# A third stack buffer, and the second of two layer norms computed from the first one's input, in a fused attention and expert kernel

## The reference

```python
# block A: x = x + difference attention to the context; layer norm without weights
h  = _layernorm(x)                       # "B1", this h is also the residual's base
# token block, entered with h
n1 = _layernorm(h, ln1_g, ln1_b)         # "B": a norm of something already normed
h  = h + softmax(causal(q(n1) k(n1)^T / 4)) v(n1) Wp + bp      # 16 heads, T = 1024
n2 = _layernorm(h, ln2_g, ln2_b)         # "M"
h  = h + top-2-of-8 experts(n2)          # each expert 256 -> 1024 -> 256 with gelu
# later blocks: C (attention), L1 (ternary), D, L2 (butterfly weights), E, F (routed attention)
```

## Time and profile before

| | us |
|---|---|
| median of three runs | 4305.14 |
| the three runs | 4296.96, 4305.14, 4316.94 |
| the profiled execution | 4313.47 |
| its span from first to last instruction | 4311.7 |
| mean granted TensorE clock | 0.915 |

### The profile page before, as it was taken

One profiled execution on the slowest core, in us unless ns is written; L12 is line 12 of the kernel. 1 busy time (PEld: TensorE's weight loads), 2 busy tenths in 40 slices (PEclk: granted clock), 3 DMA queues, 4 the chain that ended last, 5 costly groups with the idle time before them and its releaser, 6 DMA issues.

```text
span 4311.7 us, 55263 instructions
## 1 busy us (share of the span) xinstructions
PE 3544.3 (82%) x21566; PEld 1905.3 (44%) x21566; DVE 2280.4 (53%) x5155; ACT 1523.4 (35%) x2282; POOL 353.6 (8%) x270
## 2 busy tenths in 40 slices
PE   5388878878878849999779798797987988888889
PEld 2233333343343338888435334453344543444534
DVE  8865466466466436666463443724446344364343
ACT  3134424334333423443342323433225332244322
POOL 6000001000100124444000000000000000000000
PEclk8688988988988869999999899899999999999989
DMA  3221231131040168777210302102120122101130
GB/s 120 84 69 16 71 94 16 53 111 16 20 145 9 27 152 221 225 224 206 55 35 21 56 12 51 35 1 39 49 51 16 21 33 55 45 16 26 26 62 11
DMA packets 206360, 279.59 MB, mean 65 GB/s; under 512 B 100816, under 2 KB 164962, under 8 KB 190116
## 3 DMA queue, kind: packets, MB, share of 16 engines
q1 hardware_dynamic: 189065, 255.41, 22.5%
q0 software_dynamic: 17024, 20.53, 2.4%
HBM read 199.30 MB, written 75.14 MB: 64 GB/s over the span
## 4 chain that ended last, share of the span: by engine, by line
PE 52%; DVE 25%; DMA 8%; ACT 7%; issue 4%; SPq 2%; POOL 1%; DVEq 0%; ACTq 0%; another core or an unknown queue 0%
PE ps L860 6%; PE ps L1365 5%; DVE max_parts L2018 4%; PE ps L807 4%; PE ps L809 4%; PE ps L808 4%; PE ps L996 3%; PE ps L956 3%; PE ps L1211 3%; PE ps L1218 3%; DMA x_tokens<-scr_x_normalised,arena 2%; PE ps L979 2%; DVE minus_max_context L2154 2%; ACT arena L1535 2%; PE ps L1139 2%
## 5 line engine op out<-in xcount | busy, mean ns | idle before, releaser
L860 PE MATMUL ps<-ternary_W,ident 128*128 128x512 f16 x2420 | 741.3, 417 | 123.7 <-ACT arena L1596 36.8
L2018 DVE TENSOR_REDUCE max_parts<-ps 128x1 f32<-128x512 f32 (+3 forms) x768 | 387.2, 552 | 210.4 <-PE ps L959 161.0
L1467 ACT ACTIVATE arena<-ps 128x256 f32<-128x256 f32 (+7 forms) x512 | 319.1, 650 | 465.1 <-PE ps L979 288.3
L860 PEld LDWEIGHTS ps<-ternary_W,ident 128*128 128x128 f16 x2420 | 239.3, 104 | 466.5 <-issue 144.1
L956 PE MATMUL ps<-k_stack,q_stack 96*128 96x512 f16 (+3 forms) x768 | 265.5, 381 | 76.6 <-DVE max_parts L2018 33.9
L1535 ACT ACTIVATE arena<-ps 77x1024 f32<-77x1024 f32 x192 | 190.4, 1016 | 273.8 <-PE ps L1131 268.8
L1938 DVE CAST arena<-arena 128x256 f16<-128x256 f32 (+3 forms) x424 | 160.8, 379 | 235.2 <-ACT arena L1633 151.1
L2432 DVE TENSOR_REDUCE max_parts<-ps 128x1 f32<-128x512 f32 x256 | 170.6, 689 | 171.9 <-PE ps L1338 169.3
L979 PE MATMUL ps<-q_stack,k_stack 98*128 98x512 f16 (+3 forms) x768 | 236.1, 353 | 30.4 <-ACT arena L1467 27.1
L1940 DVE TENSOR_TENSOR arena<-arena 128x256 f16<-128x256 f32 (+3 forms) x424 | 246.1, 580 | 14.6
L1697 ACT ACTIVATE arena<-ps 128x1024 f32<-128x1024 f32 x128 | 130.5, 1023 | 337.1 <-PE ps L1354 337.1
(11 more groups left out here) (433 smaller groups left out, 7259.4 us busy)
## 6 DMA issues: line engine op xcount, KB each, us to landing
arena<-scr_expert_weights SPq DMA_DIRECT2D x52, 1024.0 KB, 7.4
k_stack<-scr_expert_weights SPq DMA_DIRECT2D x26, 1024.0 KB, 7.6
q_stack<-in_exp_W SPq DMA_DIRECT2D x16, 1024.0 KB, 10.6
scr_expert_weights<-k_stack SPq DMA_DIRECT2D x16, 1024.0 KB, 4.9
q_stack<-scr_q SPq DMA_DIRECT2D x120, 128.0 KB, 3.9
scr_q<-arena SPq DMA_DIRECT2D x48, 256.0 KB, 2.9
k_stack<-scr_q SPq DMA_DIRECT2D x72, 128.0 KB, 4.1
scr_q<-arena SPq DMA_DIRECT2D x16, 512.0 KB, 4.2
```

The source lines that it names most:

```text
L860: pe.matmul(s[:, 0:CH], ident[:], Wq1[:, 0, 0:CH], start=True, stop=True)
L1467: act.activation(PR[:, n % NP, kt * P:T], slot(L, "ST", g, kt, j)[:, kt * P:T], ACT.Exp).then_inc(*did("act", L, "exp", g, kt, j))
L2018: dve.tensor_reduce(mpart[:, j * NT + t, c:c + 1], slot(L, "S", g, t, j, c)[:, 0:n], AX, ALU.max).then_inc(*frees("dve", L, "S", g, t, j, c))
```

## The change

It has three parts.

1. A third buffer of stacks: `Wexp` serves as its query half and `RT` as its key half. Group g uses buffer g % 3. The stack of group 2 is loaded straight after those of groups 0 and 1, ahead of the first `max_rows`; the stack of group 3 waits for the last `ST` of group 0.
2. Because `Wexp` and `RT` are overwritten, both (1 MB each) are stored to DRAM at the head of batch 0, ahead of the first expert loads in SP's list, and loaded again in phase 1 behind the weights of tiles 0 to 2. Constant rows of the third buffer are loaded once.
3. `norm_twice` replaces both calls of `norm`. The mean of a normed row is zero and its variance is v / (v + eps), so B needs no statistics of `H`: two small products, one more square root, reciprocal and product give a scale, and `XN["B"]` is computed from `X`. Its eight tiles are written first, the eight of `H` afterwards, ahead of `x_affine` in DVE's list.

```diff
+        stack_q = [QS[:, 0], QS[:, 1], Wexp[...].bitcast(F16)...]
+        stack_k = [KS[:, 0], KS[:, 1], RT[...].bitcast(F16)...]
...
             def stacks(L, own, g):
-                buf = g % 2
-                if g >= 2:
-                    sp.wait_ge(*of("pe", L, "ST", g - 2, NT - 1 if own else 0, GH - 1))
+                buf = g % 3
+                if g >= 3:
+                    sp.wait_ge(*of("pe", L, "ST", g - 3, NT - 1 if own else 0, GH - 1))
...
                 sp.wait_ge(*of("st_q1", L))
                 sp.wait_ge(*of("st_k1", L))
+                stacks(L, True, 2)
                 max_rows(L, 0)
...
-                    if g + 2 < NG:
-                        stacks(L, True, g + 2)
+                    if g + 3 < NG:
+                        stacks(L, True, g + 3)
...
             for b in range(NB):
+                if b == 0:
+                    sp.dma_start(d_up, Wexp[...]).then_inc(*did("st_l2", 0))
+                    sp.dma_start(d_down, RT[...]).then_inc(*did("st_l2", 1))
...
+                if b == 0:
+                    sp.wait_ge(*of("st_l2", 1))
+                    sp.dma_start(stack_q[2][48:MROW], A["c_qs"][:, 0])...
+                    sp.dma_start(stack_k[2][48:MROW + 2], A["c_ks"][:, 0])...
...
             for i in range(3):
                 tile_table(i)
                 tile_weights(i)
+            sp.dma_start(Wexp[...], d_up).then_inc(*did("ld_l2", 0))
+            sp.dma_start(RT[...], d_down).then_inc(*did("ld_l2", 1))
...
+            def norm_twice():
+                var2, rstd2, rboth = sm[:, 136:144], sm[:, 144:152], sm[:, 152:160]
+                for t in range(NT):
+                    dve.wait_ge(*of("dve", "B1", "bn", t))
+                    dve.bn_aggr(mv[:, t], stats[:, t])...
+                dve.wait_ge(*of("act", "B1", "sd"))
+                dve.reciprocal(rstd[:], sd[:])...
+                dve.tensor_tensor(var2, rstd[:], rstd[:], ALU.mult)...
+                dve.tensor_tensor(var2, var2, mv[:, :, 1], ALU.mult)...
+                dve.wait_ge(*of("act", "B", "sd"))
+                dve.reciprocal(rstd2, sd[:])...
+                dve.tensor_tensor(rboth, rstd[:], rstd2, ALU.mult)...
+                for N, dst, scale in (("B", XN["B"], rboth), ("B1", H, rstd)):
+                    for t in range(NT):
+                        dve.tensor_scalar(dst[:, t], X[:, t], mv[:, t, 0:1], scale[:, t:t + 1], ALU.subtract, ALU.mult)...
...
-                norm("B1", X, H)
+                norm_twice()
+                x_affine("B")
                 dve.wait_ge(*of("dve", "B1", "xn", NT - 1))
-                norm("B", H, XN["B"])
-                x_affine("B")
                 own_attention("B0", H, "M")
```

More of the change, by code:

```diff
@@ L646, in _ @@
                 led.phase, led.batch = 0, b
+                if b == 0:
+                    sp.dma_start(d_up, Wexp[:, :, :].rearrange("p k n -> p (k n)")).then_inc(*did("st_l2", 0))
+                    sp.dma_start(d_down, RT[:, :, :].rearrange("p m d -> p (m d)")).then_inc(*did("st_l2", 1))
                 for i in range(2):
@@ L721, in _ @@
                 tile_weights(i)
+            sp.dma_start(Wexp[:, :, :].rearrange("p k n -> p (k n)"), d_up).then_inc(*did("ld_l2", 0))
+            sp.dma_start(RT[:, :, :].rearrange("p m d -> p (m d)"), d_down).then_inc(*did("ld_l2", 1))
             sp.dma_start(KX[:MROW + 2], A["c_kx"]).then_inc(*did("ld_const", 0))
@@ L944, in own_attention @@
                     if g is not None:
-                        buf = g % 2
+                        buf, mbuf = g % 3, g % 2
                     if kind == "S":
@@ L950, in own_attention @@
                             pe.wait_ge(*of("ld_const", 2))
+                            if g == 2 and led.batch == 0:
+                                pe.wait_ge(*of("ld_const3", 1))
                         keys = (t + 1) * P
@@ L955, in own_attention @@
                             on_edge = c * CH + n == keys
-                            mm = pe.matmul(s[:, 0:n], QS[0:MROW, buf, j, t * P:(t + 1) * P], KS[0:MROW, buf, j, c * CH:c * CH + n],
+                            mm = pe.matmul(s[:, 0:n], stack_q[buf][0:MROW, j, t * P:(t + 1) * P], stack_k[buf][0:MROW, j, c * CH:c * CH + n],
                                            start=True, stop=not on_edge)
@@ L970, in own_attention @@
                             busy(s, 2 if g else 12)
-                            pe.wait_ge(*of(f"ld_m{buf}", L, g, 1))
+                            pe.wait_ge(*of(f"ld_m{mbuf}", L, g, 1))
                         q0_ = kt * P
@@ L978, in own_attention @@
                             edge = a == q0_
-                            mm = pe.matmul(o, KS[0:MROW + 2, buf, j, kt * P:(kt + 1) * P], QS[0:MROW + 2, buf, j, a:(c + 1) * CH], start=True, stop=not edge)
+                            mm = pe.matmul(o, stack_k[buf][0:MROW + 2, j, kt * P:(kt + 1) * P], stack_q[buf][0:MROW + 2, j, a:(c + 1) * CH], start=True, stop=not edge)
                             if edge:
@@ L1404, in _, with norm_std @@
             batch_end(act, "act")
-            def norm_std(N):
+            def norm_std(N, variance=mv[:, :, 1]):
                 act.wait_ge(*of("dve", N, "mv"))
-                act.activation(sd[:], mv[:, :, 1], ACT.Sqrt, bias=epsc[:, 0:1], scale=1.0).then_inc(*did("act", N, "sd"))
+                act.activation(sd[:], variance, ACT.Sqrt, bias=epsc[:, 0:1], scale=1.0).then_inc(*did("act", N, "sd"))
             def both(slot_):
@@ L1643, in _ @@
                 norm_std("B1")
-                norm_std("B")
+                norm_std("B", sm[:, 136:144])
                 x_affine("B", "ln1_g", "ln1_b")
@@ L1924, in both @@
                 return slot_.rearrange("p (k c) -> p k c", k=KD)
+            def norm_twice():
+                var2, rstd2, rboth = sm[:, 136:144], sm[:, 144:152], sm[:, 152:160]
+                for t in range(NT):
+                    dve.wait_ge(*of("dve", "B1", "bn", t))
+                    dve.bn_aggr(mv[:, t], stats[:, t]).then_inc(*(step("B1", "mv") if t == NT - 1 else step("B1", "ag", t)))
+                dve.wait_ge(*of("act", "B1", "sd"))
+                dve.reciprocal(rstd[:], sd[:]).then_inc(*step("B1", "rstd"))
+                dve.wait_ge(*of("dve", "B1", "rstd"))
+                dve.tensor_tensor(var2, rstd[:], rstd[:], ALU.mult).then_inc(*step("B", "squares"))
+                dve.wait_ge(*of("dve", "B", "squares"))
+                dve.tensor_tensor(var2, var2, mv[:, :, 1], ALU.mult).then_inc(*step("B", "mv"))
+                dve.wait_ge(*of("act", "B", "sd"))
+                dve.reciprocal(rstd2, sd[:]).then_inc(*step("B", "rstd"))
+                dve.wait_ge(*of("dve", "B", "rstd"))
+                dve.tensor_tensor(rboth, rstd[:], rstd2, ALU.mult).then_inc(*step("B", "both"))
+                dve.wait_ge(*of("dve", "B", "both"))
+                for N, dst, scale in (("B", XN["B"], rboth), ("B1", H, rstd)):
+                    for t in range(NT):
+                        dve.tensor_scalar(dst[:, t], X[:, t], mv[:, t, 0:1], scale[:, t:t + 1], ALU.subtract, ALU.mult).then_inc(*step(N, "xn", t))
             def x_lo(N):
```

14 lines of the change are left out of this document (10 added, 4 removed).

## The result

| | before | after |
|---|---|---|
| median, four runs of each | 4311.04 | 4240.45 |
| lowest and highest | 4296.96, 4320.47 | 4234.47, 4251.26 |
| profiled execution | 4313.47 | 4234.47 |
| its span | 4311.7 | 4232.7 |
| mean granted TensorE clock | 0.915 | 0.924 |

The ratio is 0.9838, with a 95% interval of 0.9816 to 0.9859: between 61 and 79 us less, 71 by the medians. The forecast was 4244, from a sum of -61.5, which lies at the edge of that interval.

What follows compares the result with a forecast made beforehand. PE, busy 82% of the span, was taken as the bound. -51 - 14 + 3 + 0.5 = -61.5 us takes the profiled 4313.5 to 4252, a median near 4244; own range 4230 to 4258, 8 in 10 for 4226 to 4268.

Steps and rivals of the forecast that it cites:

- Part 1: Third stack buffer, phase 0: all eight late stack waits go, with the slow clock behind them; about -51 us.
- the eight stretches: First ST to PV at kt = 2 around the late stack waits; 148.9 us in sum, forecast 12 to 13 each.
- The control: Group 0's same steps with the stack already there, 11.95 us; eight make 95.6, a difference of 53.3 us.
- the dip: Low clock from group 0's quiet end, at three of the eight groups; stays, for about 0.7 us each.
- One or two stack waits below 1 us: Waits of S for stack loads in phase 0: one or two left, instead of 10 with 31.9 us.
- Part 2: Norms B1 and B in four batches: both halves split 4.0 us sooner, -16, taken as about -14 us.
- Part 3: Saving and restoring the weights: +3 us at batch 0's expert loads and +0.5 in phase 1, together +3.5.
- ACT's second split to wait: In batch 0, ACT's second expert split shows a wait of 1 to 3 us for its load.
- the clock's part would not come back: Rival, 16%: at the late stack waits part 1 gives only 31 us; sum -41, time 4264 us.
- the stall only moves: Rival, 4%: PE waits about 4 us eight times at NB or the rows of maxima instead; -10.5, 4295 us.
- the save would cost 14 us: Rival, 10%: save and restore cost 7 us in batch 0 and 7 in phase 1; sum -51, 4254 us.
- slower: Rival, 2%: the clock's fall at phase 0's quiet group ends spreads; at 15 us each, 30 us slower, 4335.

Runs made afterwards that it cites:

- e2: The changed kernel with the two old calls of norm, so the third buffer with save and restore alone; ratio 0.9893 to the kernel before.
- e5: The changed kernel run again as it is; 4244.95 us, ratio 0.9844 to the kernel before.
- e6: The changed kernel with four tiles of H written ahead of each half of x_affine; 4239.31 us, ratio 0.9827 to the kernel before.
- e7: The changed kernel with six unread matmuls in PE's pause behind NB of groups 0 and 1; 4243.95 us, ratio 0.9844 to the kernel before.
- e8: The changed kernel with the edits of e6 and e7, and the two stores moved behind batch 0's expert loads; 4234.00 us, ratio 0.9829 to the kernel before.
- e10: The kernel before with six unread matmuls in PE's pause behind NB of groups 0 and 1; ratio 0.9999 to the kernel before.
- e1: The kernel before with norm_twice only, two stack buffers and no save or restore; ratio 0.9964 to the kernel before.
- e9: The kernel before with only the two stores in batch 0 and the two loads in phase 1 added; ratio 1.0018 to the kernel before.
- e3: The kernel before with 16 unread matmuls ahead of each of the eight late stack waits; ratio 0.9959 to the kernel before.
- e4: The changed kernel with group 3's stack issued late again, after group 1 has read its stack; ratio 0.9923 to the kernel before.

## Why the prediction was right, and where its sum was off

**Part 1, said -51.** In the places that the prediction named it measured -51.2: the eight stretches take 12.46, 11.95, 12.46, 11.95, 12.46, 11.95, 12.46 and 11.95 us, 97.6 against 148.9. The control was the right one, and so was the dip: some groups begin below full clock, and their stretches are 0.5 us longer here, where I had said 0.7. The window at the first of them:

```profile
352.00:353.00 1.00, 1.00 (x3) 0.30 (x2) 0.00 (x0) 0.99 (x2) 0.00 (x0) 0.50 0.99 238
```

It has four places in the profile, and not three; batch 0 has it too. Other profiles of the third buffer have two or three such places, of 12.45 to 13.62 us, and sums of 96.7 to 99.6 (e2, e5 to e8). One or two stack waits below 1 us were said to be left; four are, and in e2, e5 and e6 one of them, at group 0 of batch 1, takes 2.2 to 2.5 us.

What the sum lacked is a term outside these stretches. `MT` 1 to 3 fell by 57.6 us, 6.4 more than the stretches; in e5 it fell by 55.6, 3.4 more than its stretches (96.7). e7 and e10 show what it is made of: behind `NB` the clock falls in some cases and holds in others, after a pause that is 1.62 us long in both kernels. The fall is real, and it needs the pause. That it is rarer in the changed kernel goes with the stalls: in the three profiles in which PE stands still at all eight late stacks the eight places take 219.1 (before), 219.1 (e1) and 221.4 us (e9), and the clock falls in 8, 7 and 8 of them. In the six others without the filler behind `NB` they take 211.6 to 216.0 (after, e2 to e6), with 4 to 7 falls. e3 is among these, with 215.6: it has the old buffers, but fillers in the waits. These are single profiles, but the two sets don't overlap. How a stall acts on the clock some 30 us later stays open, and so does the size of this term in the whole, where filling the pause saved nothing that could be seen.

I had read the Trainium skill's page on the clock gate ("TensorE: Matmul & The Clock Gate", section "A second HAM failure mode: psum-queue depth-cycling"), which says that short pauses between groups of matmuls can make the clock swing, against 340 to 352 us of the trace alone. Behind `NB` this trace agrees with it in some executions of the place (0.50 behind a pause of 1.62 us) and not in others.

**Part 2, said -14.** Measured -14.1, -14.8 in e1 and -14.9 in e5. The working said 4.0 us for each first half and four times that, less 2 for new pauses; it was 4.2 for the `CAST`, and of it 3.0 to 4.2 arrived at the first `MT` in each batch (57.98 to 53.74 in batch 0, 58.38 to 55.38 in batch 2). That the tiles of `H` give back some 1.4 us is borne out by e6, in which half of them moved away and the `CAST` came 1.3 us sooner.

**Part 3, said +3 and +0.5.** A to B1 of batch 0 rose by 2.6. The detail was not as told: I expected only ACT's second split to wait, and the first waits longer (1.43 us, then 0.61), so both loads come late. The sentence from the Trainium skill's page "DMA: Bandwidth & Descriptors" (section "Queues, rings and completion order"), that one ring's descriptors are consumed in order, would have given just this for the first load, and e8 agrees so far: behind the loads the stores cost nothing. In phase 1 the restore shows as +0.9 us, in a spread of 4.5 between profiles. e9's +8 for both together has 3.5 within its interval of 2 to 13, but its middle lies above it.

**The rivals.** That the clock's part would not come back is refuted by the windows at 396 to 408, and e3 shows the two parts of the cost one by one. That the stall only moves is refuted by the stretches, none above 12.46 here and none above 13.62 in the other profiles of the whole change. That the save would cost 14 us is just outside e9's interval; a cost between is not excluded. Of slower there is no sign.

**The sum.** -51.2 for the stretches, -6.4 behind `NB`, -14.1 for the norms, +2.6 and about +0.5 give -68.6. The medians say -71 and -68. The forecast's -61.5 differs by the term behind `NB`, which it did not have, and the two executions shown lie 8 us further apart, since that of the changed kernel is the fastest of its four. That the time itself came out so near, 4240.45 where 4244 was said, is partly luck: the sum was 9 us short, and the three runs that it was taken from had a median 5.9 us below that of the four runs in the table.

## What to carry to other kernels

A long wait of PE is priced by the stretch around it, against the same steps without the wait in the same trace: here 4 us of waiting cost 6.7. When data can't come sooner, unread matmuls in the wait bring back what the clock takes behind it (18.4 of 22.4 us in e3, and all that was lost behind the waits). When a chain is shortened, look at what now stands ahead of its next consumer in that engine's list: the eight tiles of `H` took back a quarter of the norms' gain, and two thirds of that (3.7 of 5.6 us over four batches) came back by moving four of them.

## What the runs showed of the hardware that I had not expected

- The same pause of 1.62 us behind `NB` is followed by a clock of 1.00 in one group and of 0.50 in another, in kernels and executions alike. The place takes 25.95 us when the clock holds, and 26.6 to 28.0 when it falls.
- Keeping PE busy through all these pauses took 8 to 9 us out of the eight places (e7, e10) and nothing measurable out of the whole, whose intervals are 6 to 11 us to either side. Why is open.
- The code behind phase 1 is the same in all kernels, and takes 2241 to 2262 us from profile to profile. A difference of a few us in one profile of the whole says nothing; the cuts do, where they differ by more than other profiles do there.
